# A two-layer gated cross-attention kernel: second layer's keys and values made during routing, weights split during the experts

## The reference

```
x = x + tanh(g_xattn[0]) * xattn0(layernorm(x), ctx)   # 16 heads of 64, keys of the own batch, Wo, bo
x = x + tanh(g_ffn[0])   * moe(layernorm(x))           # router 256->8, top 2; per expert
                                                       # (silu(x W1a + b1a) * (x W1g + b1g)) W2 + b2, W1 256x1024, W2 512x256
x = x + tanh(g_xattn[1]) * xattn1(layernorm(x), ctx)   # 8 heads of 128, all 308 keys of both batches;
                                                       # sim = (sim - mean) * 1.5 + mean before the softmax; Wout, bout
x = x + tanh(g_ffn[1])   * coupling(layernorm(x))      # 3 cycles of a small gelu net and a signed permutation
```

## Time and profile before

| | |
|---|---|
| runs | 1012.08, 1014.6, 1015.47 us (median 1014.6) |
| profiled execution | 1014.85 us, of it the span 1013.0 us |
| mean granted TensorE clock | 0.952 |
| PE busy | 933.9 us (92%) |
| PEld busy | 849.0 us (84%) |
| DVE busy | 569.5 us (56%) |
| ACT busy | 468.2 us (46%) |
| POOL busy | 371.5 us (37%) |
| DMA | 76.15 MB in 37503 packets |

### The profile page before, as it was taken

How to read it: one execution, slowest core, us unless ns; L and a number is a source line. 1 busy time by engine, 2 the same in 40 slices (tenths; PEclk the granted TensorE clock), 3 DMA queues, 4 the chain that set the end, 5 groups by cost and what they waited for, 6 DMA issues and landing times.

```text
span 1013.0 us, 20489 instructions
## 1 busy us (share of the span) xinstructions
PE 933.9 (92%) x6821; PEld 849.0 (84%) x6822; DVE 569.5 (56%) x1319; ACT 468.2 (46%) x1451; POOL 371.5 (37%) x498
## 2 busy tenths in 40 slices
PE   5999999999999755999999996899999999989995
PEld 3589999999998755999999974799999999975662
DVE  7554555545455464334444346777777776663273
ACT  0255555555555211444434433656555655544442
POOL 5153343433433103222222115655555643423132
PEclk9899999999999856999999998899999999999987
DMA  9400000000000044977667733100000000000002
GB/s 280 131 1 2 1 0 1 2 1 2 1 0 1 7 167 148 319 258 251 244 244 250 255 109 106 28 22 21 13 21 10 22 1 1 2 1 1 1 0 83
DMA packets 37503, 76.15 MB, mean 75 GB/s; under 512 B 5101, under 2 KB 23777, under 8 KB 37313
## 3 DMA queue, kind: packets, MB, share of 16 engines
q1 hardware_dynamic: 34033, 66.03, 19.6%
q0 software_dynamic: 3408, 9.31, 2.7%
HBM read 66.02 MB, written 9.31 MB: 74 GB/s over the span
## 4 chain that ended last, share of the span: by engine, by line
PE 85%; DVE 8%; POOL 2%; ACT 2%; issue 1%; DMA 1%; POOLq 0%; DVEq 0%; SPq 0%; ACTq 0%
PE banks L1527 14%; PE banks L487 11%; PE banks L489 11%; PE banks L488 11%; PE banks L521 8%; PE banks L495 6%; PE banks L506 6%; PE banks L513 3%; PE banks L636 3%; PE banks L1738 2%; PE banks L353 1%; PE banks L1342 1%; PE banks L1742 1%; PE banks L1517 1%; PE banks L1724 1%
## 5 line engine op out<-in xcount | busy, mean ns | idle before, releaser
L1527 PE MATMUL banks<-region_b,region_a 128*128 128x128 f32 x1248 | 147.8, 277 | 1.1 <-ACT region_b L1560 0.5
L1527 PEld LDWEIGHTS banks<-region_b,region_a 128*128 128x128 f32 x1248 | 144.6, 194 | 1.8 <-issue 0.9
L1102 ACT ACTIVATE region_a<-banks,negmax 128x154 f32<-128x154 f32 x256 | 96.0, 388 | 91.0 <-DVE negmax L851 89.8
L1257 POOL TENSOR_TENSOR region_a<-region_a,recip 128x512 f32<-128x512 f32 x64 | 66.5, 1039 | 178.7 <-DVE recip L857 178.7
L1292 POOL TENSOR_TENSOR region_a<-region_a,recip 128x640 f32<-128x640 f32 x64 | 80.2, 1253 | 107.7 <-DVE recip L971 107.5
L1606 DVE SCALAR_TENSOR_TENSOR region_a<-banks,region_b,region_a 128x128 f32<-128x128 f32 x156 | 43.9, 345 | 108.9 <-PE banks L1527 108.9
L521 PE MATMUL banks<-region_a 128*128 128x128 f32 x768 | 96.6, 275 | 1.9 <-DVE oT_low L874 1.8
L521 PEld LDWEIGHTS banks<-region_a 128*128 128x128 f32 x768 | 91.0, 192 | 2.9 <-issue 2.2
L495 PE MATMUL banks<-region_a 128*128 128x308 f32 x256 | 77.1, 425 | 0.0
L487 PE MATMUL banks<-Wo_high,oT_high 128*128 128x256 f32 x256 | 76.0, 297 | 0.9 <-DVE oT_low L874 0.9
L1161 ACT CAST pT_high<-banks 128x640 fp32r<-128x640 f32 x64 | 44.4, 694 | 66.8 <-PE banks L636 66.8
(11 more groups left out here) (249 smaller groups left out, 2470.0 us busy)
## 6 DMA issues: line engine op xcount, KB each, us to landing
region_a<-in_L_ffn_W SPq DMA_DIRECT2D x39, 1024.0 KB
y_slots<-region_b SPq DMA_DIRECT2D x39, 128.0 KB
W<-in_L_ffn_W SPq DMA_DIRECT2D x1, 4096.0 KB, 17.4
region_b<-in_L_xattn_Wq SPq DMA_DIRECT2D x2, 1024.0 KB
xn_rows<-region_b SPq DMA_DIRECT2D x1, 2048.0 KB, 8.5
out<-x SPq DMA_DIRECT2D x4, 512.0 KB, 2.9
region_b<-in_L_xattn_Wk SPq DMA_DIRECT2D x2, 768.0 KB, 7.3
region_b<-in_L_xattn_Wv SPq DMA_DIRECT2D x2, 768.0 KB
```

The costliest lines, as they stand in the source:

```text
L1102: e = act.activation(pr[:, j, 0:L.keys], scores[:, g % 2, u, i * L.keys:(i + 1) * L.keys], ACT.Exp, bias=negmax[:, g % 2, j:j + 1], accum_ ...
L1257: pool.tensor_tensor(whole, pr[:, :, 0:split], rc.broadcast_to([P, L.hs, split]), ALU.mult)
L1527: mm = pe.matmul(banks[:, 2 * r + part, m * P:(m + 1) * P], W1[:, r, k, cols], xgT[:, r, k, :], start=(k == 0), stop=(k == DK - 1))
```

## The change

- **Loads.** Wk, Wv, Wq and Wo of layer 1 are loaded at the start, where all of W2 was loaded; after the last slot only the bias is.
- **Keys and values of layer 1.** `ctx_shifted` is made by VectorE before the first attention's loop. The 14 units are made in the routing stage: two value units behind the transpose of b1, the 8 key units and the other two value units behind the rank matmuls, the two remainder units behind the token matmuls. ScalarE copies each unit unsplit out of PSUM into `L1_raw`, where Wq and Wo lie too.
- **Splits of layer 1's weights, keys and values.** `L1_raw` (Wq, V, K, Wo) is split in ten pieces of 964 elements, one at the end of each of the rounds 1 to 10 of the experts: `piece_high` on ScalarE, then GpSimd waits for it and subtracts.
- **W2.** It is no longer split in the first attention; each slot's 0.5 MB is loaded by SyncE into a ring of three buffers (in 1 KB rows; `load_w2(j+3)` behind the store of y of slot j), cast by ScalarE (`w2_high`) and subtracted by VectorE (`w2_low`), two slots ahead of its use.
- **Passage.** What remains there is the gathers, the mixing, the normalization and the q product; the mixing of the second two tiles stands behind the first row maximum.

SBUF regions are laid out anew for this (not shown). The diff, cut to its core:

```diff
 # loads at the start (SyncE)
-            sp.dma_start(W2..., t_in["L0_ffn_W2"]...).then_inc(sem("w2_in"), 16)
+            load_keys_values(sp, 1)
+            load_attention(sp, 1)
...
 # first attention: VectorE, ScalarE
-            def W2_rest(t):
-                dve.wait_ge(sem("W2_high"), t + 1)
-                dve.tensor_tensor(tile_of(W2_low_part, t), tile_of(W2, t), tile_of(W2_high_part, t).bitcast(F32),
-                                  ALU.subtract).then_inc(sem("W2_split"), 1)
+            dve.tensor_reduce(ctx_sum, ctxT[:, :, :], AX.X, ALU.add).then_inc(sem("ctx_sum"), 1)
+            dve.wait_ge(sem("ctx_sum"), 1)
+            for at, keys in ((0, KEYS), (KEYS, 2 * P)):
+                last = dve.scalar_tensor_tensor(ctx_shifted[...], ctx_sum..., -1.0 / (3 * KEYS), ctxT[:, :, 0:keys], ...)
+            last.then_inc(sem("ctx_shifted"), 1)
...
-                            act.copy(tile_of(W2_high_part, t), tile_of(W2, t)).then_inc(sem("W2_high"), 1)
...
 # the units
+        KV1_UNITS = [("v", 0, 0), ("v", 0, 1)] + [("k", c, 0) for c in range(NC)] + [("v", 1, 0), ("v", 1, 1)] + \
+            [("r", 0, half) for half in range(2)]
+        def act_kv1(act, units):                # one unsplit copy a unit
+            for n in units:
+                kind, a, half = KV1_UNITS[n]
                 act.wait_ge(sem("kv1_ps"), n + 1)
...
+                last.then_inc(sem("kv1_raw"), 1)
...
 # routing: TensorE, GpSimd, ScalarE
+            pe_kv1(pe, (0, 1))
+            pe.wait_ge(sem("b1_ready"), 1)
             for n in range(NT + 3):
...
                 .then_inc(sem("rank_ps"), 1)
+            pe.wait_ge(sem("xet_sb"), NT)
+            pe_kv1(pe, range(2, 2 + NC + 2))
             for n in range(TOP * NT):
                 if n % 8 == 0:
                     pe.wait_ge(sem("numbered_ready"), n // NT + 1)
...
             mm.then_inc(sem("token_ps"), 1)
+            pe_kv1(pe, range(2 + NC + 2, len(KV1_UNITS)))
...
+            pool.memset(V1[:, :, 2, :], 0.0).then_inc(sem("v_zero"), 1)
...
             act.copy(b1, ...).then_inc(sem("b1_ready"), 1)
+            act_kv1(act, (0, 1))
...
+            act_kv1(act, range(2, 2 + NC + 2))
             act.wait_ge(sem("margin_ready"), 1)
             act.activation(weight[:, 1, :], weight[:, 0, :], ACT.Exp).then_inc(sem("margin_exp"), 1)
+            act_kv1(act, range(2 + NC + 2, len(KV1_UNITS)))
             act.activation(table[:, 0:1], zero_eps[:, 0:1], ACT.Silu)
...
 # experts: SyncE
+            sp.wait_ge(sem("kv1_ps"), len(KV1_UNITS))
+            for j in range(RING):
+                load_w2(j, j)
             sp.wait_ge(sem("hg_ps"), 1)
             load_w1(RING, 0)
...
                     sp.dma_start(tile_of(ys, j), y_slot[:, r]).then_inc(sem(f"ey_out{r}"), 16)
-                    if isinstance(j, int) and j == 0:
-                        sp.wait_ge(sem("xn_stored"), 16)
-                        load_keys_values(sp, 1)
+                    if is_tile(j + RING):
+                        load_w2(j + RING, r)
...
 # experts: TensorE, before the output product
-                    e = owner_of(pe, j)
+                    pe.wait_ge(sem("W2_low"), j + 1)
                     pe.wait_ge(sem("act_low"), j + 1)
...
 # experts: ScalarE
+            def w2_high(j, r, i, reused):
+                act.wait_ge(sem(f"w2_in{r}"), 16 * (i + 1))
+                if reused:
+                    act.wait_ge(sem("ey_ps"), j - 2)
+                act.copy(W2_high[:, r], W2[:, r]).then_inc(sem("W2_high"), 1)
+            def piece_high(i):
+                act.copy(tile_of(L1_high, i - 1), tile_of(L1_pieces, i - 1)).then_inc(sem("piece_high"), 1)
...
                         act_high(j + 1, after(r, 1)[0], not (isinstance(j, int) and j < 2))
+                    if is_tile(j + 2):
+                        w2_high(j + 2, after(r, 2)[0], i + after(r, 2)[1], not (isinstance(j, int) and j < 1))
+                if not isinstance(i, int) or 1 <= i <= PIECES:
+                    piece_high(i)
...
 # experts: VectorE
+            def w2_low(j, r):
+                dve.wait_ge(sem("W2_high"), j + 1)
+                dve.tensor_tensor(W2_low[:, r], W2[:, r], W2_high[:, r].bitcast(F32), ALU.subtract).then_inc(sem("W2_low"), 1)
...
                         act_low(j + 1, after(r, 1)[0])
+                    if is_tile(j + 2):
+                        w2_low(j + 2, after(r, 2)[0])
...
 # experts: GpSimd, end of a round
                     if is_tile(j + 3):
                         gather_x(r)
+                if not isinstance(i, int) or 1 <= i <= PIECES:
+                    pool.wait_ge(sem("piece_high"), i)
+                    pool.tensor_tensor(tile_of(L1_low, i - 1), tile_of(L1_pieces, i - 1), tile_of(L1_high, i - 1).bitcast(F32),
+                                       ALU.subtract).then_inc(sem("piece_low"), 1)
...
 # passage: TensorE, VectorE, ScalarE, GpSimd
-            pe_kv1(pe, "vk")
             pe.wait_ge(sem("xn_ready"), t0 + 2)
             pe_pair_x(pe)
-            pe_kv1(pe, "r")
-            pe.wait_ge(sem("Wq_split"), 2)
+            pe.wait_ge(sem("piece_low"), PIECES)
             pe.wait_ge(sem("xt2_sb"), 1)
             pe_pair_q(pe, 0)
-            pe.wait_ge(sem("kv1_sb"), KV1_BEFORE_R + 2)
...
-            dve_kv1(dve, L1, "v")
-            dve_kv1(dve, L1, "k", range(0, 4))
             mixed_pair(0)
-            dve_kv1(dve, L1, "k", range(4, NC))
...
-            dve.tensor_tensor(Wq_low[:, 1], Wq[:, 1], Wq_high[:, 1].bitcast(F32), ALU.subtract)\
-                .then_inc(sem("Wq_split"), 1)
-            dve_kv1(dve, L1, "r")
-            mixed_pair(2)
             pair_q_rest(1, 0)
             row_max(0, 0)
+            mixed_pair(2)
             pair_q_rest(2, 1)
...
-            act.copy(Wq_high[:], Wq[:]).then_inc(sem("Wq_high"), 1)
...
-            act.copy(Wo_high[:], Wo1).then_inc(sem("Wo_high"), 1)
...
-                    if first and n in (1, 2):
-                        pool.wait_ge(sem("Wo_high"), 2)
-                        part = slice((n - 1) * NC // 2, n * NC // 2)
-                        pool.tensor_tensor(Wo_low[:, part], Wo1[:, part], Wo_high[:, part].bitcast(F32),
-                                           ALU.subtract).then_inc(sem("Wo1_split"), 1)
...
-                    pool.tensor_tensor(Wq_low[:, 0], Wq[:, 0], Wq_high[:, 0].bitcast(F32), ALU.subtract)\
-                        .then_inc(sem("Wq_split"), 1)
```

More of the change, by code:

```diff
@@ L119, in flamingo @@
         W1_SIZE = E * DK * H2
-        K_low, Wo_low = split_parts(W1_SIZE - NC * (KEYS + D), K_low=[P, NC, KEYS], Wo_low=[P, NC, D])
+        PIECES = 10
+        PIECE = -(-(2 * DK * INNER + NC * 3 * P + NC * KEYS) // PIECES)
+        LOW_AT = W1_SIZE - PIECES * PIECE
+        L1_low, = split_parts(LOW_AT, L1_low=[P, PIECES, PIECE])
         BLK = 4 * P
@@ L228, in flamingo @@
         cur = late(NT * D, "p (t d) -> p t d", t=NT)
-        late(NB * DK * BLK)
         cw1 = late(DK * 256, "p (k n) -> p k n", k=DK)
@@ L249, in flamingo @@
         coef = late(NT * 4, "p (t q) -> p t q", t=NT)
[L251 removed]
+        assert at[0] <= LOW_AT
         TURNED = KEYS + 2 * P
[L254 to L255 removed]
+        Wk1, Wv1 = [w1_region[0:CK, n * 2 * INNER:(n + 1) * 2 * INNER].rearrange("p (k n) -> p k n", k=2) for n in range(2)]
+        ctx_at = 4 * INNER
+        ctx_shifted = w1_region[0:CK, ctx_at:ctx_at + 2 * TURNED].rearrange("p (k n) -> p k n", k=2)
+        ctx_sum = w1_region[0:CK, ctx_at + 2 * TURNED:ctx_at + 2 * TURNED + 2]
         Wr = sb("Wr", [P, DK, E])
@@ L421, in pe_kv1 @@
                         left = ctxT[:, k, a * P:(a + 1) * P] if kind == "v" else ctx_rem1[:, k, :]
-                        mm = pe.matmul(bank, left, Wv[:, k, half * 512:(half + 1) * 512], start=(k == 0), stop=(k == 1))
+                        mm = pe.matmul(bank, left, Wv1[:, k, half * 512:(half + 1) * 512], start=(k == 0), stop=(k == 1))
                 mm.then_inc(sem("kv1_ps"), 1)
-        def remainder_rows(j):
-            return slice(64 * j, 64 * j + 64)
-        def act_kv1(act, L, kinds, chunks=range(NC)):
-            for n, (kind, a, half) in enumerate(KV1_UNITS):
-                if kind not in kinds or a not in chunks:
-                    continue
+        def act_kv1(act, units):
+            for n in units:
+                kind, a, half = KV1_UNITS[n]
                 act.wait_ge(sem("kv1_ps"), n + 1)
-                bank = kv1_bank(n)
+                bank = banks[:, KV1_BANKS[n]]
                 if kind == "k":
-                    last = act.activation(K_high[:, a, :], bank[:, 0:KEYS], ACT.Copy, scale=L.scale)
+                    last = act.activation(K1[:, a, :], bank[:, 0:KEYS], ACT.Copy, scale=L1.scale)
                 elif kind == "v":
-                    last = act.copy(V_high[:, half * 4:half * 4 + 4, a, :], bank.rearrange("p (c n) -> p c n", c=4))
+                    last = act.copy(V1[:, half * 4:half * 4 + 4, a, :], bank.rearrange("p (c n) -> p c n", c=4))
                 else:
```

(17 more changed lines are left out.)

192 lines of the change are left out of this document (74 added, 118 removed).

## The result

The changed kernel took 1035.37 us in the median of four runs (1033.29 to 1039.13), the kernel before 1014.76 (1012.08 to 1015.47): ratio 1.0212, 95% interval 1.0177 to 1.0247. The forecast was 1009.5 us, faster, with a range up to 1022; the time lies outside it and on the other side.

What follows compares the result with a forecast made beforehand. TensorE was taken to bound the first attention and the experts, but not routing or the passage to the second attention. Terms 1.0 - 1.5 + 0.3 - 0.7 + 10 - 14.5 = -5.4 on 1014.85 gave 1009.5 us, range 998 to 1022.

Steps and rivals of the forecast that it cites:

- Experts, DMA: Expert slots: W2's added loads fit the DMA engines' time and are covered by the ring of three; 0, ends 0 and +15.
- Stall 0.95 us per round, ten rounds: +10: Experts: GpSimd's wait for ScalarE's piece delays the next gather behind W1, so TensorE stalls; +10 us, ends 0 and +25.
- Rival B: Experts: the gather falls behind W2's rows too, adding 1.5 us in each of ten rounds; 1024.5 us, chance 0.17.
- rule on the rings: Experts: by it the gather would mix with W1 and cost nothing, the sum 10 us lower; set aside on a trace.
- Rival C: Experts: DMA engines become the bound at 5.4 us per slot, gathers in time; 1006.5 us, chance 0.06.
- The mutual exclusion of VectorE and GpSimd: Experts: w2_low can add at most its own 1.2 us to GpSimd's start, pushing toward Rival B.
- Routing: Routing stage: filled gap keeps TensorE's clock up, -1.5; key and value units behind the rank matmuls, +0.3; last term, -0.7.
- The last term of routing: End of routing: remainder units fit under the gather's landing and may leave hidden(0) a higher clock; -0.7, ends -2 and +0.5.
- The passage: Last slot to second attention: faster gather and mixing, splits gone, earlier q product; -14.5 us, ends -12 and -17.
- The first attention: First attention: VectorE's added reduction and shifts ahead of the loop delay the row maximum; +1.0 us, ends 0 and 2.3.

Runs made afterwards that it cites:

- E9: E5 with layer 1's weights in 33 pieces of 296 elements, one per slot, each subtracted by GpSimd three slots after its cast: 999.0 us.
- E2: The changed kernel with eleven pieces of 880 elements, GpSimd subtracting each a round after ScalarE's cast, so it never waits; W2's traffic whole: 1017.13 us.
- E11: E9 with the cast and subtraction of W2 put back to two slots ahead: 1015.39 us.
- E1: The changed kernel with W2 loaded for the first three slots only; casts, subtractions and GpSimd's wait for the piece stay: 1009.62 us.
- E5: E2 with W2 cast and subtracted a slot later, for slot j+1 instead of j+2: 1009.27 us.
- E8: E5 with the two value units moved from ahead of the router's transposes to behind the rank matmuls: 1015.59 us.
- E10: E9 with the mixing of tiles 2 and 3 put back ahead of the first q_low: 1001.8 us.
- E3: The changed kernel with the edits of both E1 and E2, no later W2 loads and pieces a round early for GpSimd: 998.49 us.

## Why the prediction was wrong

**The failed step is "Experts, DMA ... Ends 0 and +15, taken 0".** It compared rates (0.74 and 0.29 of a slot against a ceiling of 1.03 to 1.10), and the rates were right: E9 runs with a share of 1.00 and loses nothing. What it missed is who stands for the transfer. The sentence "Its weights are wanted 4 us after issue and covered by the ring of three" gave ScalarE's cast the right time and no margin. The load is issued 1.8 us after the slot's start S and the cast starts at S+5.8. By the prediction's own figures W1's data end at 3.4, and 1.5 us of W2 and 0.9 of gather and y end at 5.8 too. The ring does not help ScalarE, which casts W2 for slot j+2 those 4 us after its load was issued, behind W1 in the same queue, and has `silu` and `evacuate_x` queued behind that wait. I counted the cast's length (1.05 us; it takes 1.04) and not its wait. W2 landed 4.1 us after issue in the median, and 6.8 in the round shown. Measured without the late gather: 18.6 us (E2), of which the cast's place is nearly all (16.4 us, E11 against E9).

**The second step that failed is the size of the stall, once W2's traffic is there.** "Stall 0.95 us per round, ten rounds: +10": without W2's traffic E1 measured 0.95 each and 11.1 us in all, so the working was right for W1 alone. With W2's traffic it becomes 24.7 us of waits and about 9 us of half clock (six slots of 6.5 to 6.9 us) behind the severe ones: 34 us, where the prediction's end was +25 for a gather "served behind W2 too". Rival B had this shape, a gather behind W2's rows, but not this cause. It named a race with the W2 load of the same slot, to be lost once ScalarE or GpSimd is 0.5 us late. In the changed kernel GpSimd's subtraction ends 10.9 us after S (the slot's start, 460.5 here) instead of 10.1, and the gather's instruction 12.2 instead of 11.7. Yet that race was won: the W2 load of that slot is late too, issued at 473.71, 1.0 us after the gather's instruction has ended. What stood before the gather was the W2 of the slot before, on its way until 474.5, and W1. B was priced at 1.5 us a round, for W2's own time on an idle machine, and 1024.5; here the gather needs up to 6.2 us, and the half clock was left out altogether. I had used just that effect of the clock in routing and did not carry it over. Both would make the 7.1 us of interaction; no run separates them.

**The Trainium skill's rule on the rings** (DMA: Bandwidth & Descriptors, Queues, rings and completion order: each engine goes round between its queue rows packet by packet) was set aside by one trace. In the changed kernel packets of both queues do run side by side from 474 us on, though none of the gather's in the 1.3 us after its instruction; how far that is the queue and how far GpSimd's making of descriptors, no run here tells. Either way the gather lost: its packets are spread from 474 to 479 us, and GpSimd and TensorE go on when the last have come.

**Rival C, the DMA engines as the bound**, was right to be small: E9 excludes it at this traffic, with 5.22 us a slot at a share of 1.00.

**The mutual exclusion of VectorE and GpSimd** was in the text, behind the Trainium skill (SBUF — State Buffer, SBUF: two separate sides: a VectorE operation with two SBUF inputs and a GpSimd one that reads SBUF shut each other out for a whole instruction), but on the wrong instruction: I let it lengthen GpSimd's start through `w2_low`. It is VectorE's `act_low` that is shut out for the whole subtraction (2.49 us for 0.68: it starts 0.14 us behind the subtraction and ends 0.56 behind its end, so the trace agrees). Its cost is 10.3 us, and only where the cast of W2 is late (E5 against E9); with the early cast no run shows any that is clear of the noise.

**What was right.** Routing: -2.9 for -1.9, and by the named cause, the clock (E8). The size is partly luck: this stretch took 42.4 us here and 37.8 to 43.7 in the other traces with the same instructions, against 45.3 before. Its rows, in the chain of waits:

```profile
359.18 3.23 PE banks L1286 x16
...
387.78 6.70 PE banks L1486 x32
```

The last 16 router matmuls take 3.23 us as in the earlier trace rows, so the clock has fallen by then, but they start 5.2 us earlier, of which 2.3 were there when the stage began. The last term of routing (-0.7, the remainder units and the clock of `hidden(0)`) had the wrong sign: `hidden(0)` took 6.70 for 5.66, which stands in the first slot of the experts. That too differs between executions: it took 3.84 in E1 and E10, 5.35 in E5 and 5.46 in E3 and E9. The passage: -12.5 for -14.5. The chain there:

```profile
633.99 0.43 DVE region_b L1612
...
640.98 2.88 DMA W<-y_slots,slot_now
...
643.89 0.49 DVE x L801
...
644.41 0.48 DVE x L801
...
653.92 0.70 DVE q_low L930
...
669.78 0.76 PE banks L615 x5
```

The last gather lands 2.88 us after its issue (forecast 3.02, before 6.02), the two mixing steps take 0.49 and 0.48, the third transposes of probabilities start 35.8 us after the last y (633.99 to 669.78; forecast some 35, before 47). Of the missing 2 us 0.8 lie ahead of that transpose and the rest behind it; they were not traced further. The first attention: the first row maximum comes 2.56 us earlier than before (32.81 for 35.37), the third 1.75, and from the seventh on it is 2.31, as at the stage's end. So the shift of the context cost 0.8 us on the way and 0.25 in the end, not +1.0. The 2.56 us ahead of it go with TensorE's clock, 1.00 in the changed kernel and 0.55 before in 30 to 35 us. That differs between executions (E3 has 0.69 there and was only 1.2 us ahead), and I take it to belong to no edit.

## What to carry to other kernels

A transfer costs what the engine that stands for it has queued behind: look for the wait of each instruction that reads a fetched buffer, in its engine's order, and not for the bandwidth or the depth of the ring. Put such reads as late in the order as their users allow, and work that GpSimd and VectorE both do in SBUF in pieces shorter than the slack of the chain beside it. The first uses up the slack that the second needs: late reads with long pieces left 10.8 us above the floor (E5), short pieces with early reads 16.9 (E11). With both, and with GpSimd's pieces some slots behind ScalarE's casts, the whole change works: E9 takes 999.0 us, 0.987 of the kernel before and 36 us below the changed one.

## What was not expected of the hardware

- Weights read with a stride of four 4-byte columns: 328 ns per load for 192, 397 per matmul for 275: 138.5 us more than E5 in all. The Trainium skill (SBUF — State Buffer, Door 1: The DMA port swizzle) says that SBUF has lines of 16 bytes and that each access which crosses to a new line pays a penalty; a stride of four float32 opens a new line each time, and these two rows agree with that. The Trainium skill gives, at the same place, four float32 as how far one can stride for free; here a stride of four was not free.
- A DMA share of 1.00 at 345 GB/s for 180 us with TensorE busy in all of them (E9).
- After a standstill of 4.35 us the granted clock was 0.75 on the mean in the next slot, which took 1.6 us more; behind the six standstills of 2.15 to 4.35 us it was 1.3 to 1.7 us. Those of about 1 us cost 0.06 us in it (E1: 5.26 to 5.28 us in the slots behind).
- The granted clock differs between executions of the same instructions. In 352 to 356 us, in routing, it was 1.00 in E3 and 0.64 in E9, and the stretch from the transpose of b1 to the first turn took 37.8 and 43.2 us. The spread of a kernel's runs goes with it: the fastest run of E9, 995.1 us, had a mean granted clock of 0.967, the slowest, 1008.5, one of 0.953. That is more than E10 could resolve.
